# Edge matrices: one add and one report a group in place of two

## The reference, cut to what matters

```
counts[dst, src]  = number of edges from src to dst      (layers 0 and 1)
weights[dst, src] = sum of edge_weight of those edges    (layer 2)
layer 0: gamma = segment_sum((x @ wn)[dst], src) / number of edges of src
layer 2: out   = segment_sum(norm * (x @ W)[row], col) + b,  norm from edge_weight and its column sums
```

## Time and profile before

| | us |
|---|---|
| median of 3 timed runs | 3310.27 |
| the 3 timed runs | 3297.1, 3310.27, 3316.18 |
| profiled execution, its own time | 3282.36 |
| its span in the trace | 3280.7 |
| stage of `edge_matrices` in it (first L573 to end of last L590) | 499.25 to 850.97 |

### The profile page before, as it was taken

How to read it: one execution, slowest core, us unless ns; L and a number is a source line. 1 busy time by engine, 2 the same in 40 slices (tenths; PEclk the granted TensorE clock), 3 DMA queues, 4 the chain that set the end, 5 groups by cost and what they waited for, 6 DMA issues and landing times. The chain is left out here.

```text
span 3280.7 us, 46641 instructions
## 1 busy us (share of the span) xinstructions
PE 2659.8 (81%) x13179; PEld 2008.8 (61%) x13179; DVE 2267.9 (69%) x4898; ACT 1587.8 (48%) x3520; POOL 1295.7 (39%) x1269
## 2 busy tenths in 40 slices
PE   5515979999898799986879998678799999978677
PEld 3304864444447688863868886346577767756565
DVE  8304999999773488854348884566688888885646
ACT  1104988999422377640247663121445555544241
POOL 4774000000170366643047674333666666630101
PEclk9756989999998899998889999888899999988888
DMA  2000000000334345421344434403677777860101
GB/s 77 2 2 12 1 1 0 0 0 0 95 112 153 106 132 141 126 87 70 147 125 137 126 118 76 107 35 125 222 237 239 244 241 241 222 141 1 42 26 64
DMA packets 120972, 330.79 MB, mean 101 GB/s; under 512 B 23271, under 2 KB 37546, under 8 KB 120814
## 3 DMA queue, kind: packets, MB, share of 16 engines
q0 software_dynamic: 60000, 172.83, 18.4%
q1 hardware_dynamic: 60814, 156.07, 14.8%
HBM read 243.04 MB, written 85.77 MB: 100 GB/s over the span
## 5 line engine op out<-in xcount | busy, mean ns | idle before, releaser
L1636 POOL DMA_INDIRECT x_got<-table_dram,src_idx x376 | 404.6, 1076 | 220.6 <-DVE msg L1748 117.8
L702 POOL DMA_INDIRECT feature_rows<-in_edge_attr,ids x376 | 370.1, 984 | 117.4 <-issue 111.9
L705 POOL COPY ids<-id_idx 128x136 uint32 (+2 forms) x5 | 1.2, 245 | 917.4 <-DVE id_idx L798 593.5
L632 PE MATMUL bank<-hot_src,hot_dst 128*128 128x417 bf16 x1728 | 330.7, 343 | 22.2 <-ACT hot_dst L613 15.8
L613 ACT ACTIVATE hot_dst<-hot_dst,slot_w 128x128 bf16<-128x128 bf16 x1080 | 327.1, 387 | 22.9 <-DVE hot_dst L573 21.8
L496 PE MATMUL bank<-row_hot,col_part 125*128 125x432 f32 x920 | 205.0, 384 | 143.5 <-DVE row_hot L390 84.9
L1215 DVE TENSOR_TENSOR pt_low<-bank,pt_high 128x640 fp32r<-128x640 f32 x320 | 249.7, 819 | 86.2 <-ACT pt_high L1179 70.9
L496 PEld LDWEIGHTS bank<-row_hot,col_part 125*128 125x128 f32 x920 | 176.0, 200 | 173.0 <-DVE row_hot L390 91.6
L632 PEld LDWEIGHTS bank<-hot_src,hot_dst 128*128 128x128 bf16 x1728 | 157.5, 98 | 195.2 <-ACT hot_dst L613 62.1
L1209 DVE CUSTOM_DVE_ANT_0 p<-bank,log_counts 128x1254 f32<-128x1254 f32 x160 | 232.8, 1455 | 49.0 <-PE bank L1116 46.1
L1179 ACT CAST pt_high<-bank 128x640 fp32r<-128x640 f32 x320 | 208.2, 696 | 119.2 <-PE bank L1132 106.1
(11 more groups left out here) (415 smaller groups left out, 6689.5 us busy)
## 6 DMA issues: line engine op xcount, KB each, us to landing
features_dram<-feature_parts POOLq DMA_DIRECT2D x94, 512.0 KB
edge_got<-features_dram SPq DMA_DIRECT2D x94, 512.0 KB
qk_dram<-qk_high SPq DMA_DIRECT2D x16, 640.0 KB, 2.9
qk_dram<-qk_low SPq DMA_DIRECT2D x16, 640.0 KB, 4.2
keys<-qk_dram SPq DMA_DIRECT2D x32, 320.0 KB
queries<-qk_dram SPq DMA_DIRECT2D x32, 320.0 KB
queries_low<-qk_dram SPq DMA_DIRECT2D x32, 320.0 KB
at_dram<-at_rows SPq DMA_DIRECT2D x10, 640.0 KB, 5.6
```

Source lines behind the costliest of these rows:

```text
L632: m = pe.matmul(k.bank[:, 2 * u + c, 0:C3], hot_dst[:, u, j, q, :], hot_src[:, u, j, 0:C3], start=(j == 0 and q == parts[0]), stop=(j == G ...
L702: pool.indirect_dma_start(out=rows[:, g % 2, j * ED:(j + 1) * ED], out_offset=None, in_=self.a.edge_attr_128, in_offset=bass.IndirectOffse ...
L1636: pool.indirect_dma_start(out=xg[:, g % XRING, j, :], out_offset=None, in_=k.table_dram, in_offset=bass.IndirectOffsetOnAxis(ap=k.src_idx[ ...
```

## The change

`acc_c` and `acc_a` become the two halves of one SBUF array `acc` at the same addresses. `add` on DVE becomes one instruction over 2 x 417 elements, from two PSUM banks into both halves. PE raises one semaphore a group, `group_done`, after the weights, and waits once a group for `added`. The starting values and multiples of the semaphores are scaled to that. The number, shapes and order of the matmuls, the hot matrices and the copies of ACT stay.

```
-                dve.wait_ge(added, g * 2 + 4)
-                for c, acc in enumerate((acc_c, acc_a)):
-                    dve.wait_ge(chunk_done, g * 2 + c + 5)
-                    rows = acc[:, bass.ds(to, C3)]
-                    dve.tensor_tensor(rows, k.bank[:, 2 * u + c, 0:C3], rows, ALU.add).then_inc(added, 1)
+                dve.wait_ge(added, g + 2)
+                dve.wait_ge(group_done, g + 3)
+                rows = both[:, :, bass.ds(to, C3)]
+                dve.tensor_tensor(rows, k.bank[:, 2 * u:2 * u + 2, 0:C3], rows, ALU.add).then_inc(added, 1)
...
-                    act.wait_ge(chunk_done, g * 2 + 2)
+                    act.wait_ge(group_done, g + 1)
...
                     pe.wait_ge(hots_built, g * (GT + 1) + GT + 1)
+                    pe.wait_ge(added, g + 1)
                     for c, parts in enumerate(((0,), (1, 2, 3))):
-                        pe.wait_ge(added, g * 2 + c + 1)
                         if c:
                             pe.wait_ge(weighted, g + 1)
...
-                        m.then_inc(chunk_done, 1)
+                    m.then_inc(group_done, 1)
...
-    k.acc_c = r.take("acc_c", [P, NB, NP], F32)
-    k.acc_a = r.take("acc_a", [P, NB, NP], F32)
+    k.acc = r.take("acc", [P, 2, NB, NP], F32)
+    k.acc_c, k.acc_a = k.acc[:, 0, :, :], k.acc[:, 1, :, :]
```

More of the change, by code:

```diff
@@ L558, in edge_matrices @@
     S = nc.alloc_semaphore
-    hots_built, chunk_done, added = S("hots_built"), S("chunk_done"), S("chunk_added")
+    hots_built, group_done, added = S("hots_built"), S("group_done"), S("group_added")
     weighted = S("hots_weighted")
@@ L563, in edge_matrices @@
     hot_dst = r.take("hot_dst", [P, 2, GT, 4, P], BF16)
-    acc_c, acc_a = (m[:].rearrange("p b n -> p (b n)") for m in (k.acc_c, k.acc_a))
+    both = k.acc[:].rearrange("p a b n -> p a (b n)")
     with nc.Block() as block:
@@ L584, in add @@
                 to = dve.value_load(k.place3[0:1, bass.ds(g, 1)], min_val=0, max_val=(NB - 1) * NP + 2 * C3)
-                dve.wait_ge(added, g * 2 + 4)
-                for c, acc in enumerate((acc_c, acc_a)):
-                    dve.wait_ge(chunk_done, g * 2 + c + 5)
-                    rows = acc[:, bass.ds(to, C3)]
-                    dve.tensor_tensor(rows, k.bank[:, 2 * u + c, 0:C3], rows, ALU.add).then_inc(added, 1)
-            dve.sem_inc(added, 4)
+                dve.wait_ge(added, g + 2)
+                dve.wait_ge(group_done, g + 3)
+                rows = both[:, :, bass.ds(to, C3)]
+                dve.tensor_tensor(rows, k.bank[:, 2 * u:2 * u + 2, 0:C3], rows, ALU.add).then_inc(added, 1)
+            dve.sem_inc(added, 2)
             build(0, 0)
@@ L618, in _ @@
         def _(pe):
-            pe.sem_inc(chunk_done, 4)
+            pe.sem_inc(group_done, 2)
             with pe.Fori(0, NG3 // 2) as i:
```

## The result

The changed kernel took 3339.45 us in the median (4 runs, 3334.74 to 3341.59), the kernel before 3307.69 us (4 runs, 3297.1 to 3316.18). The ratio is 1.0085, with a 95% interval of 1.0064 to 1.0107: 28 us slower, between 21 and 35; the two medians themselves lie 31.8 us apart. The forecast was 23.5 us more and 3333.

The account below looks back on a forecast made before the run. A closed ring of waits over DVE, ACT and PE was taken as the bound; the merged add's 0.435 us on 54 laps gave 23.5 us, 3310.3 + 23.5 = 3333.8, called 3333, range 3312 to 3350.

Parts of the forecast that it names:

- The add: DVE's merged add of 834 elements takes about 1.02 us, 0.435 more a lap on the ring, 23.5 us in all.
- The other links: From DVE's build to ACT's start 0.39 us, ACT's ten copies 3.08, PE's 12 matmuls 2.43, all unchanged.
- the ring: Closed chain of waits DVE add, build, ACT copies, PE matmuls; two groups grow from 6.41 to 6.85 us.
- The single wait of PE: PE waiting once a group for `added`: taken as 0, low end 16 us less.
- The single report: ACT's wait at L609 asks for all of group g-2 in both versions, so it is never last: no term.
- The registers: DVE's address work behind the wait: 0 to 0.05 us a lap, 3 us at most, taken as 0.
- The later stages: Semaphore scaling and the merged array change no address or instruction there; all other stages as before.
- Part of the add stays hidden: Rival: DVE's and PE's savings return on the ring, lap grows by 0.2 us, 11.6 us in all, 3322; chance 0.13.
- DVE's throughput is the bound: Rival: DVE's queue sets the pace, 0.07 us less a group, 7 us in all, 3303; chance 0.05.
- L446's pace: Rival: DVE's add runs at the strided SBUF pace, 62 us more, 3372; chance 0.06 together with low clock.
- The low clock: Rival: PE's clock falls, 2.0 us a lap, 110 us if throughout, 3444; chance 0.06 together with strided pace.
- What would show it: Signs in the changed profile: add about 1020 ns, DVE idle about 0.4 us every group, PE near 89%, stage 375 us.

Follow-up runs that it names:

- the repetition: The changed kernel timed again against the kernel before on a second chip, no edit: ratio 1.0081 (1.0067 to 1.0095), stage 24.0 us longer.
- the run with the counts alone: The changed kernel with one add of 417 elements a group, the sums of the weights left out: lap 6.43 us, stage 351.5 us.
- four pairs of banks: The changed kernel with four PSUM bank pairs for two, building group g+2 before adding group g: lap 5.97 us, ratio 0.9923 to the kernel before.
- the run with the hot matrices first: The changed kernel with DVE building the four destination matrices of group g+2 before the wide add of group g: lap 7.05 us, stage 386.7 us.

## Why the prediction was right

Its sum holds term by term. The add: 1026 ns for 1020, and the first build of the next group (L573 before, L574 after) follows 0.94 behind for 0.945. The other links: 0.39, 3.08 and 2.45 for 0.39, 3.08 and 2.43. The lap: 6.86 for 6.85. The stage, 54 laps: 24.0 us longer for 23.5. The interval of the measured 28 us (21 to 35) holds the 23.5, and so does that of the 24.5 us of the repetition (20 to 29). That the median came out 6 us above the 3333 is nothing that the sum speaks of: executions of one kernel lie further apart than that on the first chip. That the ring, and not DVE's throughput, set the pace was argued from DVE's and ACT's idle times; the run with the counts alone shows it, since there DVE has half the adding and the lap does not move.

The terms that I set to nothing were nothing. The single wait of PE: shown alone. The single report: shown with 417 elements. The registers: no more than the 0.01 by which the lap exceeds the sum. The later stages: the repetition's ratio leaves no more than a few us for them.

The rivals fell. "Part of the add stays hidden" asked for a lap near 6.6. "DVE's throughput is the bound" is false in both kernels and true in the one with four pairs of banks, where one instruction less gives 0.063 us a group, against 0.07 in my text. The Trainium skill (VectorE: DVE Perf Modes, "The TRN2 errata — SBUF-src ops pay a fixed extra latency per instruction") advises tiles of 512 elements and more. That pair of runs agrees with it, by 0.063 us a group; the kernel before and the changed one do not, since there the merged add made the stage 24.0 us longer. The clock stayed at 1.00 from 510 us to the stage's end with PE at 91% and with pauses in each group, so the swing that the Trainium skill describes (TensorE: Matmul & The Clock Gate, "A second HAM failure mode: psum-queue depth-cycling") did not come. L446's pace did not come either.

Two prices of rivals were wrong, without effect on the forecast. The low clock was priced by the 12 matmuls on the ring alone, 110 us. At 0.35 us a matmul the 32 of two groups would take 11.2 us, more than the lap of 6.85, so PE itself would be the bound: 54 x (11.2 - 6.85) is an estimate of 235 us more. And the price of L446's pace uses 1.85 ns an element for one piece and 1.95 for the other; with the 1.81 that 935 ns for 432 elements leave, it is 58 us rather than 62. ACT's 6.08 us for 20 copies was too high as well, as the run with four pairs of banks showed; it lay below the lap either way.

One step of "What would show it" was wrong in form: DVE and ACT do not idle 0.4 us in every group but 0.8 in every second. Both rings have the lap 6.86. The second one runs as close behind the first as DVE's work allows (700.35 to 703.34 is 2.99, which is 0.94 + 2.05), so all slack gathers on the other side: 6.86 - 2.99 = 3.87, of which 0.8 is idle. The kernel before had the same, 3.06 and 3.35. PE's share was 90.7% rather than 89.

## What to carry to other kernels

Two adds of which the first overlaps the producer are not the same as one wide add behind the last report: find what waits for the instruction that follows, and count the elements between the producer's last result and that instruction. Merge instructions on an engine only where its own queue is the bound; here that came with more PSUM buffers and the build ahead of the add, and with them the same merge gained. When three engines are near 95% and none is at 100%, add up a closed chain of starts over one lap; it gave this result to 0.01 us.

## What was not expected of the hardware

A load of a place into a register cost DVE nothing while its sequencer did it ahead of the wait for PE, and 0.58 us of idle time in half of the groups when it stood behind that wait; moving it ahead of the wait shortened the lap by 0.64 us. In the run with the hot matrices first the sequencer's own rows at the load (L591) are 0.30 us for the load and mostly 0.19 for a register operation behind it:

```profile
L591 DVEq FUSED_REGOPS  x214: 53/190/210, 364.0 to 738.2; - x107
L591 DVEq TENSOR_LOAD <-place x108: 299/305/567, 364.1 to 737.9; - x108
```

The instruction behind a wide add starts before the add ends in the trace: 0.94 us after the start of an add of 1.026 us.
